# Reordering the queues of three attention phases, with the norm applied by ScalarE

## The reference

```python
x = x + xattn(layernorm(x), context)     # attention 0: 16 heads of 8, q from x, k and v from context
x = x + expert_choice(layernorm(x))      # not touched
# decoder block on layernorm(x):
sa = mha(n, n, causal_mask);  n = layernorm(n + sa, g1, b1)      # attention 1: self attention
ca = mha(n, context, pad_mask); n = layernorm(n + ca, g2, b2)    # attention 2: cross attention
ff = relu(n @ w1 + b1) @ w2 + b2;  x = x + layernorm(n + ff, g3, b3)
x = x + moe(layernorm(x))                # not touched
```

## Time and profile before

| what | us |
|---|---|
| median of 3 runs | 2280.21 (2277.04 to 2282.47) |
| the profiled execution | 2276.67 |
| its span, first to last instruction | 2274.7 |
| attention 0, 1, 2, in the span | about 24 to 379, 689 to 1061, 1068 to 1402 |
| PE / DVE / ACT / POOL busy, share of the span | 89% / 76% / 45% / 23% |
| granted TensorE clock, mean | 0.95 |

### The profile page before, as it was taken

One profiled execution on the slowest core, in us unless ns is written; L12 is line 12 of the kernel. 1 busy time (PEld: TensorE's weight loads), 2 busy tenths in 40 slices (PEclk: granted clock), 3 DMA queues, 4 the chain that ended last, 5 costly groups with the idle time before them and its releaser, 6 DMA issues. The chain is left out here.

```text
span 2274.7 us, 52942 instructions
## 1 busy us (share of the span) xinstructions
PE 2021.8 (89%) x19268; PEld 1557.3 (68%) x19268; DVE 1738.6 (76%) x4586; ACT 1015.3 (45%) x1956; POOL 511.8 (23%) x504
## 2 busy tenths in 40 slices
PE   5999995777777999997999997994999999999998
PEld 3666664566664666664677675764888888888887
DVE  4767766677755888887799995665888888888886
ACT  3455452445542444443455553543444444443443
POOL 0101100000001222322122222663222232232221
PEclk9999998899996999998999998996999999999999
DMA  3000000000000000000000001000000000000000
GB/s 121 20 28 28 18 18 1 1 1 0 0 1 1 1 0 0 0 0 19 30 28 28 28 18 63 1 0 0 6 6 10 5 5 10 5 5 9 6 5 10
DMA packets 27248, 30.41 MB, mean 13 GB/s; under 512 B 1936, under 2 KB 20624, under 8 KB 26896
## 3 DMA queue, kind: packets, MB, share of 16 engines
q1 hardware_dynamic: 27152, 29.28, 4.1%
HBM read 25.08 MB, written 4.19 MB: 13 GB/s over the span
## 5 line engine op out<-in xcount | busy, mean ns | idle before, releaser
L320 ACT ACTIVATE ex<-ps 128x512 f32<-128x512 f32 x384 | 228.7, 596 | 335.7 <-PE ps L580 334.5
L1102 ACT ACTIVATE moe_sg<-ps 128x512 f32<-128x512 f32 x288 | 172.6, 599 | 365.0 <-PE ps L1154 364.8
L414 DVE TENSOR_REDUCE mx<-ps 128x8 f32<-128x512 f32 x384 | 262.5, 684 | 62.0 <-PE ps L562 61.2
L580 PEld LDWEIGHTS ps<-pack,sh 128*128 128x128 f32 x1536 | 173.9, 144 | 185.0 <-DVE sh L416 113.3
L580 PE MATMUL ps<-pack,sh 128*128 128x128 f32 x1536 | 253.7, 289 | 44.4 <-DVE sh L416 43.1
L1138 PEld LDWEIGHTS ps<-down,moe_act 128*128 128x128 f32 x2048 | 266.1, 191 | 33.9 <-DVE moe_acc L1331 13.0
L1138 PE MATMUL ps<-down,moe_act 128*128 128x128 f32 x2048 | 271.0, 275 | 7.3 <-DVE moe_acc L1331 7.3
L416 DVE TENSOR_TENSOR sh<-ps,mx 128x512 f32<-128x512 f32 x384 | 265.6, 692 | 13.2
L596 PEld LDWEIGHTS ps<-vblk,ex 128*64 128x64 f32 x6144 | 215.1, 140 | 66.8 <-issue 66.2
L596 PE MATMUL ps<-vblk,ex 128*64 128x32 f32 x6144 | 258.1, 228 | 0.3
L1313 DVE TENSOR_TENSOR moe_act<-ps,moe_sg 128x512 f32<-128x512 f32 x288 | 197.7, 686 | 69.2 <-PE ps L1154 55.2
(11 more groups left out here) (232 smaller groups left out, 3663.7 us busy)
## 6 DMA issues: line engine op xcount, KB each, us to landing
ctxT<-in_ctx SPq DMA_DIRECT2D x32, 256.0 KB, 2.8
x_res<-in_x SPq DMA_DIRECT2D x16, 256.0 KB, 2.9
kmi<-in_key_mask SPq DMA_DIRECT2D x16, 256.0 KB, 3.4
out<-moe_acc SPq DMA_DIRECT2D x16, 256.0 KB, 2.3
pack<-in_pack SPq DMA_DIRECT2D x1, 2536.5 KB, 9.2
wqkv<-in_wqkv SPq DMA_DIRECT2D x1, 1536.0 KB, 8.5
gate<-in_gate SPq DMA_DIRECT2D x6, 192.0 KB, 4.0
up<-in_up SPq DMA_DIRECT2D x6, 192.0 KB, 4.1
```

The lines of the kernel that those rows point to most:

```text
L320: nc.scalar.activation(ex[:, u % 2], UB[u % 4].rearrange("p (c n) -> p c n", n=P), ACT.Exp).then_inc(e_ready, 1)
L414: nc.vector.tensor_reduce(mx[:, u % 2], sc, AX.X, ALU.max).then_inc(max_done, 1)
L580: last = nc.tensor.transpose(UB[u % 4][:, c * P:(c + 1) * P], sh[:, u % 4, c * P:(c + 1) * P], ident)
L1102: nc.scalar.activation(sg[:, k % 2], GB_[k % 2], ACT.Silu).then_inc(silu_done, 1)
```

## The change

In the DVE list every `shift` becomes the first work of its slot, and the rest moves behind it and mostly later: `residual` of the two halves from slots 0 and 4 to 2 and 6, `divide` of the second half of group g-1 from 2 to 3 and of the first half of g from 6 to 7, `normalise` from 2 and 6 to 4 (attention 1: 5) and 7, the key mask from 0 to 1. `norm_apply` leaves DVE. ACT applies the norm instead in slot 2, as `rstd * x + (-mean * rstd)`; DVE adds one small operation (negmean) and POOL one (nmr). On PE, `make_onT` moves from slots 2 and 6 to 4 and the next step's 0, `project` from 3 and 7 to 5 and the next step's 1; `copy_onT` on ACT follows. The rounds of attention 1 move from slots 2, 3, 4, 7 to 3, 4, 5, 7, and the four copies of k are made two and two, in two slots.

```diff
-        slots = dict(zip(rounds, (0, 3, 4, 6) if cross else (2, 3, 4, 7)))
+        slots = dict(zip(rounds, (0, 3, 4, 6) if cross else (3, 4, 5, 7)))
-        spread_at = {k_slot: (0,), k_slot + 1: (1, 2), k_slot + 2: (3,)}
+        spread_at = {k_slot: (0, 1), k_slot + 1: (2, 3)}
@@ gpsimd, inputs_of
+                    pool.wait_ge(rstd_done, nth(g))
+                    nc.gpsimd.tensor_tensor(nmr[:, :], negmean[:, :], rstd[:, :], ALU.mult).then_inc(nmr_done, 1)
@@ scalar
+            def norm_apply(g, s, first):
+                if not pre_norm:
+                    return
+                act.wait_ge(nmr_done, nth(g))
+                if not first:
+                    act.wait_ge(prep_ready, nth(g - 2, NP, nr("xT")))
+                    act.sem_inc(passed, 1)
+                for t in range(TILES):
+                    last = nc.scalar.activation(xn[:, s, t:t + 1, :], tiles_of(x_res, g, t, 1), ACT.Identity,
+                                                bias=nmr[:, t:t + 1], scale=rstd[:, t:t + 1])
+                last.then_inc(xn_ready, 1)
@@ scalar, step
-                    if v == 2 and not first:
-                        copy_onT(g - 1, 1)
-                    if v == 6:
-                        copy_onT(g, 0)
+                    if v in (0, 4) and not first:
+                        copy_onT(g - 1, v // 4)
                     if more:
                         prep_slot(g + 1, 1 - s, v)
+                        if v == 2:
+                            norm_apply(g + 1, 1 - s, first)
@@ vector, norm_stats
+                nc.vector.tensor_scalar(negmean[:, :], mv[:, :, 0], -1.0, None, ALU.mult)
@@ vector, step
-                    if not first:
-                        if v == 0:
-                            residual(g - 1, 1 - s, 0)
-                        if v == 2:
-                            divide(g - 1, 1)
-                        if v == 4:
-                            residual(g - 1, 1 - s, 1)
-                    if v == 6:
-                        divide(g, 0)
-                    if more and v == slots["q"] + 1:
-                        copy_q(g + 1, 1 - s)
                     shift(g, v)
                     if more and v == 0:
                         norm_stats(g + 1, 1 - s)
+                    if more and v == 1:
                         key_mask_of_next(g + 1, 1 - s)
-                    if more and v == 1:
-                        norm_apply(g + 1, 1 - s)
+                    if more and v == (5 if cross else 4):
+                        copy_q(g + 1, 1 - s)
                     if not first:
                         if v == 2:
+                            residual(g - 1, 1 - s, 0)
+                        if v == 3:
+                            divide(g - 1, 1)
+                        if v == 4 if cross else v == 5:
                             normalise(g - 1, 0)
                         if v == 6:
+                            residual(g - 1, 1 - s, 1)
+                    if v == 7:
+                        divide(g, 0)
+                        if not first:
                             normalise(g - 1, 1)
@@ tensor, step
-                    if not first:
-                        if v == 2:
-                            make_onT(g - 1, 1)
-                        if v == 3:
-                            project(g - 1, 1)
-                    if v == 6:
-                        make_onT(g, 0)
-                    if v == 7:
-                        project(g, 0, first)
+                    if not first and v in (0, 4):
+                        make_onT(g - 1, v // 4)
+                    if not first and v in (1, 5):
+                        project(g - 1, v // 4)
```

More of the change, by code:

```diff
@@ L100, in attention_phase @@
         rstd = sb("rstd", [P, TILES])
+        negmean = sb("negmean", [P, TILES])
+        nmr = sb("nmr", [P, TILES])
         mx = sb("mx", [P, 2, HH])
@@ L146, in attention_phase @@
         rstd_done = sem("rstd_done")
+        nmr_done = sem("nmr_done")
         xn_ready = sem("xn_ready")
@@ L328, in prep @@
             def prep(g, s):
+                if not cross:
+                    norm_apply(g, s, True)
                 for r in rounds:
                     if r == "xT":
+                        if cross:
+                            norm_apply(g, s, True)
                         copy_xT(g)
@@ L346, in step @@
                         exps(g - 1, UNITS - 1)
-                    if v == 2 and not first:
-                        copy_onT(g - 1, 1)
-                    if v == 6:
-                        copy_onT(g, 0)
+                    if v in (0, 4) and not first:
+                        copy_onT(g - 1, v // 4)
                     if more:
                         prep_slot(g + 1, 1 - s, v)
+                        if v == 2:
+                            norm_apply(g + 1, 1 - s, first)
                 if not more:
                     exps(g, UNITS - 1)
+                    copy_onT(g, 0)
                     copy_onT(g, 1)
@@ L465, in prep @@
                 key_mask_of_next(g, s)
-                norm_apply(g, s)
                 copy_q(g, s)
@@ L606, in make_onT, with project @@
                 last.then_inc(onT_ready, 1)
-            def project(g, m, first=False):
-                if not (first and m == 0):
-                    pe.wait_ge(resid_done, g * 2 + m)
+            def project(g, m):
+                if m == 1:
+                    pe.wait_ge(resid_done, g * 2 + 1)
                 pe.wait_ge(onT_copied, nth(g, 2, m))
@@ L648, in step @@
                     weigh(g, s, UNITS - 2, False)
+                    make_onT(g, 0)
                     weigh(g, s, UNITS - 1, False)
+                    project(g, 0)
                     make_onT(g, 1)
```

## The result

| | before | after |
|---|---|---|
| median, us | 2281.34 (2277.04 to 2287.01) | 2248.06 (2246.64 to 2248.29, 4 runs) |
| ratio of the times, 95% interval | | 0.9854 (0.9836 to 0.9873) |
| the profiled execution / its span, us | 2276.67 / 2274.7 | 2246.64 / 2244.8 |
| PE / DVE / ACT / POOL busy | 89 / 76 / 45 / 23% | 89 / 76 / 47 / 23% |
| granted clock, mean | 0.95 | 0.96 |

The change makes the kernel faster by 33 us, 1.5%. The same kernel run again gave 2247.16 (2246.19 to 2248.96), ratio 0.9852 (0.9836 to 0.9868).

What follows compares the result with a forecast made beforehand. PE was taken as the bound in attention 1 and 2, with stalls and clock falls in attention 0. Terms -13 - 9 + 4 - 18 + 2 = -34 gave 2242.7 profiled, median about 2247, range 2229 to 2272.

Steps and rivals of the forecast that it cites:

- The likeliest case: Whole kernel: faster, at about 2247 us, with the four clock falls gone; own range 2229 to 2258, chance 0.55.
- Attention 0's queue: Attention 0, slots 1 to 3: stalls of 0.95 in place of 1.85 us a step, over 15 steps -13 us.
- with T(0) and W(7) as cover: PE and ACT queues: the moved copy_onT and project were costed at nothing.
- The clock: Attention 0: the four falls of the granted clock go, -18 us.
- Attention 1: Attention 1's steps: stalls of 1.5 against 2.1 us, over 15 steps -9 us.
- Attention 2: Attention 2's steps: stalls at T(0) and slot 2 of 0.68 against 0.41 us, over 15 steps +4 us.
- The prologues: Before the first step of two phases: the norm lies bare, 1.2 us each, +2 us (bounds 0 and 5).
- The sum: Whole kernel: all terms together, -34 us against the profiled execution of 2276.7, giving 2242.7.
- The clock still falls: Attention 0: two remaining stalls in slot 3 keep the clock falling, 2265 us; chance 0.22.
- The stall only changes its name: Attention 0: clock falls remain and ACT's late norm takes the gain, xT waiting 1.45, 2278 us; chance 0.08.
- ACT bounds the preparation: ACT: four norms take 2.8 us or more and the exp behind is late, 2299 us; chance 0.07.

Runs made afterwards that it cites:

- E11: The change with project of the first half behind xT in slot 3 and its residual behind divide, in attention 2 only; 2258.45 us, ratio 0.9893.
- E4: The change plus one unread DVE addition of about 1.1 us ahead of shift(2) in attention 0; 2299.36 us, ratio 1.0086.
- E5: The change plus two smaller unread DVE additions in attention 0, ahead of shift(2) and shift(6); 2278.06 us, ratio 0.9994.
- E2: The kernel before, old order, with only the norm moved to ACT; 2273.92 us, ratio 0.9977.
- E1: The change with the new order only: norm_apply back on DVE behind shift(1), without negmean and nmr; 2257.6 us, ratio 0.9906.
- E3: The change with all queues of attention 2 in the old order; 2248.43 us, ratio 0.9861.
- E7: The change with two of attention 0's four norms on DVE and project of the first half in slot 2; 2254.46 us, ratio 0.9885.
- E9: E8 plus unread warm-up matmuls in the preparation of attention 2 and six behind attention 1; 2243.37 us, ratio 0.9821.
- E10: E8 plus unread warm-up matmuls in the first preparation of all three attention phases; 2233.35 us, ratio 0.9795.
- E8: E7 combined with E3's old order in attention 2, against the change; 2244.15 us, ratio 0.9843.

## Why the prediction was right, and where it was not

The forecast was 2247 (2229 to 2272), 0.84 for faster (its cases add up to 0.85); the median is 2248.06. The likeliest case came, none of the rivals did. By its steps, in the order of the sum:

**Attention 0's queue, forecast -13, measured -11.** The stalls: T(2) 0.40 (forecast 0.40), xT 0.36 (0.55): the norms begin 0.19 us before T(2) does, where the prediction had them begin with it. Four norms in a row last 1.67 us on the timeline above and one takes 0.503, where the prediction built 1.7 and 0.50 from three rows of other shapes. The groups of ACT by shape, after:

```profile
L293 ACT ACTIVATE xn<-x_res,nmr,rstd 128x128 f32 x112 | 46.3, 503 | 0.0
```

By the formula of the Trainium skill, ScalarE: Activation LUTs, section What ACT_TABLE_LOAD costs, which gives an activation a fixed part of 186 ns, 93 ns for each per-partition operand and 0.833 ns for each element of a row, the estimate is 479 ns; the row's 503 is 5% above it. The step, however, is 19.45 (19.31 and 19.59 in turn), not 19.3. Two things were missing: 0.28 at the step's boundary in every second step, and about 0.2 for the place of `project`. E11 measured that 0.2 in attention 2 alone; here it is what is left of the step, carried over. The sentence of the prediction that failed is the one that costed `project` at nothing, "with T(0) and W(7) as cover": it hides no wait, but its place on PE has a price.

**The clock, forecast -18, measured -17.8**, all four falls, and in 20 us windows from 40 to 340 us the clock is 1.00 throughout. E4 and E5 bear out the reason: at the same amount of idle in a step, how close together it stands decides. Before had 1.85 us in slots 1 to 3, E4 about 1.4 in one place, and both have four falls; E5 has E4's amount in two places 10 us apart and none. E2, with as much as before and one fall, shows that this is no sharp rule. The Trainium skill, TensorE: Matmul & The Clock Gate, section A second HAM failure mode, has PE idling briefly between groups of matmuls as enough to make the clock swing; E4's and before's windows agree. Another 3.4 us of gain was not forecast: before, the clock is 0.83 between 40 and 60 us, in the first steps, and 1.00 after. Whether the order did this is open, as E1, with the same order, has 0.74 there.

**Attention 1, forecast -9, measured -7.2.** T(0) 0.44 (0.55), T(2) and T(6) 0.41 (0.40 each), xT 0.11 (0.15): 1.37 against 1.5. The four stalls are all where they were put and no larger. The step is 21.61 and not 21.5, so the work between them is 20.24 and not 19.96, and that is the term that was mis-sized. It was a remainder, a step less stalls read from start times. That the new places of `project` and of the rounds made it longer is likely, and not tested in this phase.

**Attention 2, forecast +4, measured +8.7.** This is the term that missed most. T(2) 0.41 and, for T(0), 0.24 in one step and 0.28 at the boundary in the next: 0.67 against the forecast 0.68. But the step rose by 0.45, not by 0.27. The missing 0.2 is again `project`, 3 us in 15 steps, shown by E11; the other 2 us lie in the start and the end of the phase.

**The prologues, forecast +2:** the first `scores` of attention 0 comes 1.5 us later (1.2 forecast). The preparation of attention 1 lies in the column "choice", 315.1 against 315.2, which differs by up to 6.7 us between kernels, so its 1.2 can't be told. Nothing is seen of nmr (0.20 us each on POOL), negmean (0.17) or `xb`.

**The sum** was -34 against the profiled execution and -30.0 was measured. The forecast came within 1 us of the median because the old profile stood 3.5 under its median and the new one only 1.4: the closeness is partly luck. The sum itself was helped too: its own terms, as measured above, give -11 - 7.2 + 8.7 - 17.8 + 1.5 = -26, and most of the other 4 lie where nothing was forecast (3.4 in attention 0's first steps, 1.1 behind attention 2). And up to 10 us more depend on the starts: E3, E7 and E11, which each improve a step, did not come out faster than the change, because the change happens to have short low-clock stretches there.

**The rivals.** *The clock still falls*: no, though E4 shows how near it is, as one filler of about 1 us brings all four back. *The stall only changes its name*: xT waits 0.36 for ACT, not 1.45. *ACT bounds the preparation*: refuted with the norm at 0.50; ACT is 60% busy in attention 0 (156.38 of 260). By the rule of the Trainium skill, ScalarE: Activation LUTs, section Rules for kernel authors, the move alone would lose. E2 agrees in the step of attention 0 (+0.18 us) and shows next to nothing in attention 1 (+0.02); on top of the new order the move neither wins nor loses (change against E1: +0.30 us a step in attention 0, -0.28 in attention 1).

## What to carry to other kernels

When an engine's queue is reordered, count PE's idle not only by its sum but by how much of it stands together: 1.4 to 1.85 us within a few microseconds cost four times 4.5 us of clock in 13 steps here (in E2 only once), and 1.4 us in two halves 10 us apart cost no fall in 13 steps. Compare versions by the steady step and by start and end of each phase, from the trace, before believing a total: three edits here (E3, E7, E11) made their step shorter, as worked out, and the total did not show it. And an operation that hides no wait still has a price by its neighbour on PE (0.2 us a step for `project`).

## What was not expected of the hardware

**The clock comes back late, and at very different times.** When a phase starts after waits of PE, the granted clock is 0.50. In the first steps PE is then busy nearly all of the time, and the clock rises 4 to 28 us after the first `scores`. Attention 2's start before, in after and in E5, windows of PE alone (the first `scores` are at 1084.9, 1047.5 and 1069.9):

```profile
1088.00:1092.00 4.00, 3.89 (x32) 0.77 0.07 22
```

```profile
1052.00:1056.00 4.00, 3.63 (x54) 0.98 0.02 9
```

```profile
1092.00:1096.00 4.00, 4.00 (x37) 0.50 0.00 0
1096.00:1100.00 4.00, 4.00 (x48) 0.75 0.31 100
```

The code of attention 2 is the same in after and E5, and so are its 13 steps (259.7 and 259.8); the start costs 36.9 and 47.0. It repeats in one kernel (after and after again) but not always (E11's runs). What decides it was not found; E9 and E10 did not settle it.

**The granted clock at the start of the program is not to be trusted.** In the first steps of attention 0 the column reads 1.00, but the durations are those of the low clock. In after, the sixteen matmuls of `scores` at two times, the clock column being 1.00 at both:

```profile
32.23 1.98 PE L574 MATMUL ps<-kblk,qd 32*64 32x256 f32 x16
...
60.86 1.09 PE L574 MATMUL ps<-kblk,qd 32*64 32x256 f32 x16
```

1.98 us against 1.09. E10's matmuls are as slow in this stretch, and there the column says so, where E3's, with as many matmuls, does not. Windows of PE, E3 first:

```profile
28.00:36.00 8.00, 7.22 (x29) 1.00 0.20 66
```

```profile
28.00:36.00 8.00, 7.22 (x29) 0.54 0.22 66
```

In after this ends at about 38 us; in E3 it lasts to about 51 and in E5 to about 60, which is what makes their starts 5 and 10 us longer. In before, E1, E7 and E8 it ends by about 38 too, and the clock falls at about 42 and comes back at about 50, this time in the column (E1: 0.51 in the window from 40 to 44). That is most of what makes the starts of E1, E7 and E8 4 to 5 us longer than the change's.
